# In the second edge stage of a graph network kernel, two of three gathers wait for a step of VectorE

## What is computed

```python
k = typed_linear(x, Wk, bk); q = typed_linear(x, Wq, bq); v = typed_linear(x, Wv, bv)
att = (q[edge_dst] * key_e).sum(-1) * rel_pri[edge_type] / sqrt(dk)   # key_e: k of the source, by kind of edge
seg = edge_dst * r + edge_type
amax = segment_max(att, seg)
ex = exp(att - amax[seg])
hsum = segment_sum(w[:, :, None] * val_e, seg)      # w = ex / its segment sum, val_e: v of the source
```

## Time and profile before

| | |
|---|---|
| timed runs | 3860.44, 3868.23, 3869.61 us; median 3868.23 us |
| span of the profiled execution | 4615.6 us |
| VectorE busy | 3304.8 us (72%) |
| TensorE busy, matmuls | 3712.7 us (80%) |
| ScalarE busy | 2826.0 us (61%) |
| GpSimd busy | 2481.9 us (54%) |
| DMA queues | gathers and scatters 41.3%, SyncE's 26.2% of the 16 engines' span |
| gathers of the second edge stage | 912, from 2333.9 to 4247.5 us |

### The profile page before, as it was taken

One profiled execution on the slowest core, in us unless ns is written; L12 is line 12 of the kernel. 1 busy time (PEld: TensorE's weight loads), 2 busy tenths in 40 slices (PEclk: granted clock), 3 DMA queues, 4 the chain that ended last, 5 costly groups with the idle time before them and its releaser, 6 DMA issues. The chain is left out here.

```text
span 4615.6 us, 113336 instructions
## 1 busy us (share of the span) xinstructions
PE 3712.7 (80%) x25474; PEld 2978.4 (65%) x25475; DVE 3304.8 (72%) x10411; ACT 2826.0 (61%) x8685; POOL 2481.9 (54%) x2605
## 2 busy tenths in 40 slices
PE   4967777787778777788868888888888888888897
PEld 3545666665656565566647776676776777676797
DVE  6756666676666666655558888788888888778675
ACT  3744555564555555544448777777777777777454
POOL 3645555565555545444445555555555555555576
PEclk8978888898888888889979889899889888889899
DMA  4876666676676666666667767777767776676564
GB/s 131 257 226 203 204 198 197 197 227 195 200 209 195 203 196 198 160 208 226 231 190 201 201 197 197 197 197 201 198 197 199 199 201 196 188 199 176 190 207 143
DMA packets 613511, 915.39 MB, mean 198 GB/s; under 512 B 210712, under 2 KB 422794, under 8 KB 612916
## 3 DMA queue, kind: packets, MB, share of 16 engines
q0 software_dynamic: 168160, 579.41, 41.3%
q1 hardware_dynamic: 445268, 335.07, 26.2%
HBM read 739.98 MB, written 177.47 MB: 199 GB/s over the span
## 5 line engine op out<-in xcount | busy, mean ns | idle before, releaser
L906 POOL DMA_INDIRECT kv<-kv_table,rec x864 | 901.1, 1043 | 796.4 <-DVE msg L1042 517.6
L1574 POOL DMA_INDIRECT kv1c<-kv_table,rec x912 | 894.1, 980 | 552.3 <-DMA par<-in_par 301.1
L1619 ACT ACTIVATE wv<-kv1c,wv 128x64 f32<-128x64 f32 x3648 | 903.9, 335 | 16.0
L944 ACT ACTIVATE gates<-gates_p 128x512 f32<-128x512 f32 x864 | 474.8, 595 | 685.7 <-remote 410.5
L1682 DVE CUSTOM_DVE_ANT_0 masked_scores<-score_p,far 126x384 f32<-126x384 f32 x1216 | 604.7, 553 | 276.6 <-DMA q_blk<-q_table 137.4
L1774 PE MATMUL sum_p<-wv,hot 128*126 128x260 f32 x1824 | 581.8, 464 | 2.1 <-ACT wv L1619 2.1
L1085 PE MATMUL qe_p<-q_blk,hotT 126*128 126x256 f32 x1728 | 309.7, 328 | 252.6 <-issue 137.4
L1739 PE MATMUL qe_p<-qrel,hotT 126*128 126x256 f32 x1824 | 484.4, 404 | 23.6 <-ACT hotT L1604 17.9
L1096 PE MATMUL sum_p<-msg,hot_weighted 128*126 128x256 f32 x1728 | 469.7, 418 | 16.2 <-issue 10.6
L1764 PE MATMUL peak_p<-peak,hotT 126*128 126x4 f32 x1824 | 253.5, 256 | 268.6 <-DVE peak L1697 147.9
L1764 PEld LDWEIGHTS peak_p<-peak,hotT 126*128 126x128 f32 x1824 | 234.6, 196 | 359.0 <-issue 184.9
(11 more groups left out here) (285 smaller groups left out, 7397.1 us busy)
## 6 DMA issues: line engine op xcount, KB each, us to landing
key<-segment_keys SPq DMA_DIRECT2D x304, 189.0 KB
q_blk<-q_table SPq DMA_DIRECT2D x216, 256.5 KB
acc_table<-acc SPq DMA_DIRECT2D x304, 128.0 KB
qrel<-q_by_relation SPq DMA_DIRECT2D x304, 126.0 KB
feat<-in_edge_feat_t SPq DMA_DIRECT2D x216, 128.0 KB
agg_and_x_plus_h<-total SPq DMA_DIRECT2D x216, 126.0 KB
kv1c<-kv_table,rec POOLq DMA_INDIRECT x912
kv<-kv_table,rec POOLq DMA_INDIRECT x864
```

The source lines that it names most:

```text
L906: pool.indirect_dma_start(kv[it.slot(AHEAD)][:, t, :], None, c["kv0_d"], bass.IndirectOffsetOnAxis(ap=rec[k][:, t, 0:1].bitcast(I32), axis ...
L944: act.activation(gates[k][:, t, :], gates_p[t][:], ACT.Silu).then_inc(gates_ready, 1)
L1574: pool.indirect_dma_start(kv[k][:, t, :], None, c["kv1_d"], bass.IndirectOffsetOnAxis(ap=rec[k][:, t, 0:1].bitcast(I32), axis=0)).then_inc ...
L1619: ins = act.activation(wv[k][:, t, h, 0:DK], kv[s][:, t, D + h * DK:D + (h + 1) * DK], ACT.Copy, scale=wv[k][:, t, h, DK:DK + 1])
```

## The change

Two of the three gathers of each chunk get a wait (and the increment of `held` that follows waits here). In turn T, t = 1 waits for `qk_ready` of chunk T-2, and t = 2 waits for `peak_ready` of chunk T-3. Nothing else differs: the number and the order of the gathers, their buffers and all other engines' instructions stay.

```diff
--- before.py
+++ after.py
@@ -1571,6 +1571,12 @@
                     wait(pool, wv_ready, it, U)
                     pool.sem_inc(held, 1)
                     for t in range(T1):
+                        if t == 1:
+                            wait(pool, qk_ready, it, 2)
+                            pool.sem_inc(held, 1)
+                        if t == 2:
+                            wait(pool, peak_ready, it, 3)
+                            pool.sem_inc(held, 1)
                         pool.indirect_dma_start(
                             kv[k][:, t, :], None, c["kv1_d"],
                             bass.IndirectOffsetOnAxis(ap=rec[k][:, t, 0:1].bitcast(I32), axis=0)
```

## The result

The change makes the kernel slower by 0.7%: 3894.54 us (median of 6 runs, 3888.55 to 3904.15) against 3868.92 us of the kernel before on the same chip (6 runs, 3857.01 to 3875.49), a ratio of 1.0068 (95% interval 1.0049 to 1.0087), so 26 us more. It lies within the range of the prediction, but the forecast was "no change", and that was wrong.

What follows compares the result with a forecast made beforehand. The prediction took the exchange of VectorE and TensorE as the bound, with GpSimd and the gathers beside it. All terms on the path were 0, giving 3868 us; own range 3857 to 3880, 8 in 10 for 3841 to 3898.

Steps and rivals of the forecast that it cites:

- rival 5: Rows of the delayed t = 2 land late for qk, some 20 turns by 1 us: 3885 us, chance 0.04.
- if t = 2 starts 0.15 us after peak at the earliest: Third gather on GpSimd: with this start after its wait, delays add up to 108 us over the stage, 0 on the path.
- The landing: Rows of t = 2 before qk of chunk T: 5.4 to 9 us from peak, a delayed gather has 5.3 us; sum 0.
- Path cost of the held gather: GpSimd behind the held t = 2: 8.6 us of delay reach the fade, whose cover leaves 0 us on the path.
- t = 1 binds next to never: Second gather on GpSimd: starts before its qk is done in 1 of 302 turns, in the start-up.
- instructions of the waits cost nothing: Two waits and two increments a turn on GpSimd: taken as 0.1 us a pair, covered, so 0 on the path.
- hot isn't the loser of a lock: VectorE's hot beside a gather: the gather pays, hot nothing; the opposite rival gave 3915 us, chance 0.03.
- the gathers over 1.2 us that the prediction expected: GpSimd: t = 2 begins within hot more often, giving more gathers over 1.2 us, 0.4 us paid by the gather.
- Rival 1: GpSimd's turn becomes the bound, 5.4 us against a timed turn of 5.3: 3898 us, chance 0.09.
- Rival 2: GpSimd's fade moves onto VectorE's capped or off it: 3890 us, chance 0.07, or 3846 us, chance 0.08.
- Rival 3: VectorE's stalls at the masked scores shrink, 127 us at stake: a quarter gives 3841 us, all 3761; chance 0.13.
- spread evenly: Second edge stage: if the span-to-timed difference, ratio 0.838, is spread so, the profile's 6.3 us turn becomes some 5.3 us.

Runs made afterwards that it cites:

- experiment 2: Only the wait of t = 1 for qk added to the kernel before: 3869.66 us, ratio 1.0004.
- experiment 4: Both waits added to the kernel before, but at a lag of 8 chunks each, so always met: 3863.44 us, ratio 0.999.
- experiment 1: The kernel before, unchanged, run again for a profile in the condition of the timed runs: 3868.49 us, ratio 0.9999, span 3862.4 us.
- experiments 9 and 10: One gather more ahead of the first chunk of the kernel before, without and with the wait of t = 2 for peak, other chip condition: 4544.07 and 4427.44 us.
- experiment 10: One gather more ahead of the first chunk and the wait of t = 2 for peak, against the kernel before, other chip condition: 4427.44 us, 0.9761.
- experiment 7: Only t = 2 waits, for the second of the four maxima ahead of peak, against the kernel before: 3862.43 us, ratio 0.9989.
- experiments 3 and 8: Only t = 2 waits, against the kernel before: for peak, 3892.87 us, 1.0075; for drop_ready, the next but one instruction behind peak, 3933.77 us, 1.0187.

## Why the prediction was wrong

**The time.** 3868 was forecast, 3887 to 3895 was measured. The prediction gave the mechanism that the runs show, rival 5, "late landing", a chance of 0.04 and 3885 us. That this came near by its number (20 turns by 1 us) is luck, as the turns are others: nine of them, with 1.3 to 2.4 us ahead of qk and more behind it.

**The step that failed: "if t = 2 starts 0.15 us after peak at the earliest".** That term had no row of its own; I took 0.15 us as what GpSimd does from a release. The rows show 0.78 us in every held turn and 3.06 or 3.07 us in the nine. The prediction never asked what a gather's preparation takes when nothing hides it. The 0.30 us between two gathers in the earlier trace rows is not the whole preparation but what sticks out from beneath the gather before.

**The landing.** My own numbers with the right start give the result. From the end of peak to qk pass 5.4 us at the least, 4.8 us are needed. With a start at 0.15 that leaves 0.5 us; at 0.78 it leaves 4.6, so -0.2; at 3.06 it leaves 2.3 us, and 2.5 us are missing. Measured were 1.3 to 2.4. (The upper end of the 5.4 to 9 us is wrong, as it is 14.1 in the trace of before, but nothing rests on it.) So the slack was read at its minimum but against a start that doesn't occur. The Trainium skill ("DMA: Bandwidth & Descriptors", section "Anatomy of one DMA — SWDGE (gpsimd) path") gives about 2.0 us and bytes/436e3 for such a DMA, so for 128 rows of 2 KB an estimate of 2.0 + 0.6 = 2.6 us; the trace needs 4.9 us from the start of t = 2 to its reader in the turn of chunk 99, behind two other gathers and the loads of SyncE. By the packets, the last of t = 2 ends 3.0 us after the gather's start at the least and 3.9 us in the middle turn of the changed kernel. The measurement decides; by the page's figure the nine, with 2.3 us to go, would have been 0.3 us late and no more.

**What is given back later.** Path cost of the held gather was put at 0, with "the next fade and then the next chunk's gathers" behind it. That the fade has cover was nearly right (it makes the sum wait 0.1 to 0.4 us in six of the nine turns, where the prediction had 0). Missing was what a wait of VectorE can do to TensorE: idle for part of a turn, then 1.2 GHz, for 6.8 us after chunk 99. The nine waits account directly for 16.6 - 3.8 = 12.8 us of VectorE; the turns round them lost 17 to 22 us, a sum that one profile tells to some 10 us.

**Right were**: t = 1 binds next to never (once, 0.81 us; experiment 2 shows no cost); instructions of the waits cost nothing (experiment 4; taken 0.1 us a pair, not visible); hot isn't the loser of a lock.

```profile
L1658 DVE SCALAR_TENSOR_TENSOR hot<-iota,par,rec x304: 598/606/615, 1883.2 to 3541.2; 128x378 f32<-128x378 f32 x152
```

Its longest is 0.615 us, though hot begins while a gather runs in 273 of the 304 turns. The lock of the Trainium skill ("SBUF — State Buffer", section "SBUF: two separate sides") thus takes nothing from hot. That t = 2 begins within hot more often was wrong, by the same 0.15 us: 48 gathers t = 2 do so in experiment 1 and none in the changed kernel, as hot ends before 0.78 us have passed. So the gathers over 1.2 us that the prediction expected weren't there either (longest 1.142 us, 1.239 in experiment 1), and the change tells nothing of a gather that begins within hot. Rival 1: GpSimd's turn is not the bound; it idles 262.7 us ahead of the fade, 300.5 in experiment 1, while its idle time ahead of gathers rose from 266.8 to 336.4 us. Rival 2: capped sums to 61.0 us, against 64.4; in the second profile of the change 64.5.

**Rival 3 and the scale.** That the ratio of 0.838 between span and timed runs is "spread evenly" was wrong for the steps of a turn. It fits the middle turn (6.07 us from qk to qk in the profile of before, 5.23 in experiment 1), but the difference stands mostly ahead of one instruction: over the stage VectorE idles 276.6 us ahead of the masked scores in the one and 58.1 in the other, which is 218 of the 295 us that the stage differs by. The least time from the end of peak to qk is 5.46 us in both. So the 0.84 was not to be put on a slack ("it has 4.5 where the landing may also be shorter"), and rival 3 had nothing to gain in the timed runs. In the other condition its gain is there: with the wait 4427 instead of 4544 us (experiments 9 and 10). The reading that running ahead was "its result" only was too strong there: with less running ahead, the idle time halves (from 288 to 152 us over the stage). By what path isn't shown.

**What stays open.** What happens every 31 chunks ahead of t = 2. That nine turns carry nearly the whole price is read from timelines (20.2 of 19.4 us, 16.8 of 16.0, 22.5 of 32.4, each to some 10 us) and from the idle time ahead of their qk, but no run took these nine out alone; experiment 10 was meant to, and experiment 7 freed the other held turns as well. A share of the other held turns isn't excluded. What stretches SyncE's instructions in the other condition stays open too.

## What to carry to other kernels

A wait ahead of a DMA on GpSimd can cost its preparation too, and not only the time until the release: price it by a gather whose engine had stood idle until its release, and add the rarest, longest gap ahead of such a gather in the trace. Set that start against the landing, in the turn with the least slack, and where slack is short, issue the gather earlier in the turn instead of holding it: the order alone gave 0.4% here, and with it the waits were free. When the profile's span and the timed runs differ by more than a per cent, first find which groups hold the difference, and don't read a chance from stalls that the timed runs may not have.

## What the runs showed of the hardware

- A gather behind a wait that blocks starts 0.78 us after the step it waits for has ended (2439.42 in the changed kernel); behind another gather, with the wait met, 0.30 us after that one. With waits that are always met the gap stays 0.30 us (experiment 4).
- Every 31st chunk, from chunk 37 on, GpSimd took 0.95 us instead of 0.30 ahead of the third gather (1.14 in experiment 4, with met waits), and 3.06 or 3.07 us from the release where the wait blocked (changed kernel, experiments 3 and 8). One gather more at the start didn't move it (experiments 9 and 10).
- A DMA that lands late can stand under "issue" ahead of its reader: 1.89 us before qk at 2434.28. The gather's last packet tells: it ended 0.41 us before that qk, and 4.48 us after the gather's start.
- After TensorE had been busy 1.33 of 3 us, its granted clock was at 0.50 for 6.8 us. The wait of 1.9 us made a turn of 7.4 us, and the low clock behind it one of 7.9, where the middle turn takes 5.2.
- A hot that begins while a gather runs isn't longer than others: 0.615 us at the most, in 273 turns of the changed kernel.
- In another condition the same kernel takes 4537 instead of 3868 us, SyncE's semaphore instruction takes up to 0.72 us (1.4 in the profile of before) instead of 0.017, and the wait of t = 2, beside one gather more, makes the kernel 2.4% faster instead of 0.7% slower (experiments 9 and 10).
